# An eight-chunk decoder layer: two groups of row transposes and one copy of probabilities moved in the attention turn's hand-written order

## The reference, cut to what matters

```python
x = x + recurrence(layernorm(x))
q = layernorm(x) @ Wq + bq                      # 16 heads of 32
scores = einsum('bhqd,bhkd->bhqk', q, k) / sqrt(32)
scores = where(causal mask, -inf, scores)
out = einsum('bhqk,bhkd->bhqd', softmax(scores), v)
x = x + out @ Wo + bo
x = x + experts(layernorm(x))                   # top 2 of 4 by x @ gate_W
```

## Time and profile before

| | |
|---|---|
| median of 3 runs | 1167.13 us (1164.18 to 1169.15) |
| the profiled execution's own time | 1170.26 us |
| its span (first to last instruction) | 1168.5 us |
| PE busy | 95% of the span |
| DVE busy | 78% |
| ACT busy | 62% |
| POOL busy | 34% |
| granted TensorE clock | 0.991 of full speed |

### The profile page before, as it was taken

How to read it: one execution, slowest core, us unless ns; L and a number is a source line. 1 busy time by engine, 2 the same in 40 slices (tenths; PEclk the granted TensorE clock), 3 DMA queues, 4 the chain that set the end, 5 groups by cost and what they waited for, 6 DMA issues and landing times.

```text
span 1168.5 us, 24237 instructions
## 1 busy us (share of the span) xinstructions
PE 1108.3 (95%) x6017; PEld 905.0 (77%) x6018; DVE 910.5 (78%) x2172; ACT 722.2 (62%) x2148; POOL 393.4 (34%) x328
## 2 busy tenths in 40 slices
PE   6999999999989999999999888999999999999993
PEld 5888888888877787777777666777888888888882
DVE  6888888887874778878878877877777777777774
ACT  5223332233377777768676644866787787877873
POOL 3000000000034433545536364445534434443432
PEclk9999999999999999999999998999999999999998
DMA  8544545445340133143143377786555454444543
GB/s 261 163 149 159 190 148 173 151 163 207 126 147 1 57 89 111 56 124 100 46 145 90 128 206 219 201 249 152 94 85 81 81 85 80 86 81 81 88 63 40
DMA packets 95316, 144.76 MB, mean 124 GB/s; under 512 B 20864, under 2 KB 37428, under 8 KB 94607
## 3 DMA queue, kind: packets, MB, share of 16 engines
q1 hardware_dynamic: 77338, 106.83, 28.8%
q0 software_dynamic: 17216, 35.73, 17.4%
q10 hardware_dynamic: 693, 1.36, 0.4%
HBM read 82.69 MB, written 64.76 MB: 126 GB/s over the span
## 4 chain that ended last, share of the span: by engine, by line
PE 72%; DVE 9%; issue 7%; DMA 6%; ACT 3%; POOL 2%; DVEq 0%; POOLq 0%; ACTq 0%; SPq 0%
PE banks L1126 27%; PE banks L716 17%; PE banks L928 7%; PE banks L781 6%; DMA out<-rows,scatter_rows 4%; PE banks L893 3%; PE banks L906 3%; PE banks L1154 2%; PE banks L1138 2%; ACT rows L1335 2%; DVE operands L1615 2%; PE banks L917 1%; PE banks L754 1%; DVE rows L1917 1%; ACT operands L1218 1%
## 5 line engine op out<-in xcount | busy, mean ns | idle before, releaser
L1126 PE MATMUL banks<-operands 128*128 x1608 | 390.5, 398 | 9.2 <-ACT operands L1218 5.0
L1126 PEld LDWEIGHTS banks<-operands 128*128 128x128 f32 x1608 | 299.5, 190 | 73.9 <-issue 14.2
L716 PE MATMUL banks<-operands 128*128 128x512 f32 (+2 forms) x1224 | 290.1, 393 | 3.6 <-DVE operands L1615 3.6
L716 PEld LDWEIGHTS banks<-operands 128*128 128x128 f32 (+1 forms) x1224 | 226.1, 192 | 48.3 <-DVE operands L1615 3.7
L1218 ACT ACTIVATE operands<-banks 128x512 fp32r<-128x512 f32 (+1 forms) x232 | 137.6, 602 | 63.4 <-PE banks L807 34.2
L1615 DVE TENSOR_TENSOR operands<-banks,operands 128x512 fp32r<-128x512 f32 (+1 forms) x232 | 156.7, 683 | 15.6 <-ACT operands L1218 12.2
L1335 ACT ACTIVATE rows<-banks,score_shift 128x77 f32<-128x77 f32 x512 | 158.4, 337 | 11.2 <-DVE score_shift L1839 10.9
L2686 POOL DMA_INDIRECT out<-rows,scatter_rows x67 | 106.4, 1588 | 155.3 <-DVE rows L2419 109.7
L1218 ACT ACTIVATE operands<-rows 128x512 fp32r<-128x512 f32 (+2 forms) x77 | 54.0, 710 | 163.6 <-DVE rows L1686 139.4
L1540 ACT ACTIVATE banks<-banks,param_cols 128x128 f32<-128x128 f32 x268 | 99.2, 431 | 82.2 <-PE banks L1154 75.6
L2357 DVE BATCH_NORM_STATS2 moe_stats<-banks 128x6 f32<-128x512 f32 x134 | 93.2, 696 | 37.5 <-PE banks L1126 31.5
(11 more groups left out here) (191 smaller groups left out, 1603.1 us busy)
## 6 DMA issues: line engine op xcount, KB each, us to landing
expert_parts<-operands SPq DMA_DIRECT2D x32, 512.0 KB, 3.0
operands<-expert_parts SPq DMA_DIRECT2D x8, 2048.0 KB, 11.4
rows<-in_x SPq DMA_DIRECT2D x8, 1024.0 KB, 5.5
rows<-in_L_ffn_W SPq DMA_DIRECT2D x32, 256.0 KB, 3.6
x_rows<-rows SPq DMA_DIRECT2D x8, 1024.0 KB, 4.3
rows<-x_rows SPq DMA_DIRECT2D x8, 1024.0 KB, 6.2
xf_rows<-rows SPq DMA_DIRECT2D x32, 256.0 KB
out<-rows SPq DMA_DIRECT2D x32, 256.0 KB
```

Of the source, the lines that this page charges most:

```text
L716: last = nc.tensor.matmul(dst, stationary(a, k), moving(b, k), start=(t == 0 and k == 0), stop=(t == len(terms) - 1 and k == n_k - 1))
L1126: last = nc.tensor.matmul(dst, stationary[:, a, k, :], weights[:, w, bass.ds(e, 1), a2, k, :].rearrange("p e f -> p (e f)"), start=False, ...
```

## The change

Three lists are edited, all inside `b_turn`. On PE, the transposes of x2 go in front of the projection of tile 3, and those of x3 in front of attend(c, 0). On ACT, the high parts of x2 and x3 each go in front of one more tile of exponentials. On DVE, the low part of x2 goes in front of x2_stats(2), x2_add(3) and x2_stats(3); and near the end of the turn the copy of head 3's probabilities of group 3 goes in front of the last part of `slots` and of q_lo(c + 1, 3). No instruction is added or removed, and no DMA is moved.

```diff
@@ PE, b_turn
                 scores(c, 2, (2, 3))
-                x1_to_features(c + 1, c, (1,))
+                x1_to_features(c + 1, c, (1, 2))
                 if back:
                     project(c - 1, c, 3)
-                x1_to_features(c + 1, c, (2,))
+                x1_to_features(c + 1, c, (3,))
                 attend(c, 0)
-                x1_to_features(c + 1, c, (3,))
                 probs_to_keys(c, 1, 0)
@@ ACT, b_turn
                 exp_scores(c, 2, (1,))
+                x1_hi(c + 1, (2,))
                 exp_scores(c, 2, (2,))
-                x1_hi(c + 1, (2,))
+                x1_hi(c + 1, (3,))
                 exp_scores(c, 2, (3,))
-                x1_hi(c + 1, (3,))
                 pT_even(c, 1, 0)
@@ DVE, b_turn
                 if back2:
                     read_positions(c, totals=totals)
+                x1_lo(c + 1, (2,))
                 if back:
                     x2_stats(c - 1, c, 2)
                     x2_add(c - 1, c, 3)
-                x1_lo(c + 1, (2,))
-                if back:
                     x2_stats(c - 1, c, 3)
                 x1_lo(c + 1, (3,))
@@ DVE, b_turn, near its end
                 invert_sums(c + 1, 0)
+                pT_odd(c, 3, 1)
                 if back2:
                     slots(c - 2, c, parts=(2,))
                 q_lo(c + 1, 3)
-                pT_odd(c, 3, 1)
                 max_scores(c + 1, 1, 0)
```

## The result

| | before | changed |
|---|---|---|
| median of 6 runs | 1168.14 us (1163.45 to 1170.20) | 1181.10 us (1178.20 to 1183.26) |
| profiled execution | 1170.26 us | 1180.26 us |
| its span | 1168.5 us | 1178.5 us |
| mean granted TensorE clock | 0.991 | 0.984 |

The ratio is 1.0116, with a 95% interval of 1.0089 to 1.0143: the changed kernel is slower by 13 us, where 3.3 us of gain were forecast.

A forecast was written before the change was run, and what follows sets the result against it. PE, busy 95%, was taken as the bound, idling behind DVE at two places. Six turns at 0.55 us gave 3.3, the swapped copy nothing: 1167.13 - 3.3 = 1163.8 us, range 1158.2 to 1169.4.

The forecast's parts named there:

- x2 didn't hold up the projection: On PE, x2's transposes, now ahead of the projection, find x0 read in time, with 0.08 us to spare; costed at nothing.
- p11: Transposes of probabilities on PE, waiting for x1_lo(3): to start 0.55 us earlier in turn 4, where 1.48 were lost.
- Turn 4 stood for the others: Turn 4's gain of 0.55 us was taken for each of six turns: 3.3 us; turn 1 maybe less, turn 6 more.
- The pair x2_add, x2_stats: Dependent neighbours on DVE, put directly behind each other: 0.85 us from start to start, against 0.60 for independent ones.
- rival 3: On DVE, x2_stats directly behind x2_add costs nothing extra: 1.5 us more gain, 1162.3 us; chance 0.06.
- (1): The whole wait at p11 on PE goes: 8.9 us gained, 1158.2 us; chance 0.12.
- (2): The swapped copy of head 3's probabilities pays too, at attend(c, 3): 5.6 us in all, 1161.5 us; chance 0.07.
- (4): The gain is absorbed by a later PE wait, above all at attend(c, 3): time stays at 1167.1 us; chance 0.14.
- (5): On PE, x2's transposes hold up the projection: slower, 1173 us if 1.75 us late; chance 0.05.
- the 0.99: Part of turn 4's 1.48 us loss shown as PE idle before p11; most of the rest was put before p10.
- The bank argument: At the turn's end, attend(c, 3) needs both the probabilities' copy and q_lo, which frees its bank; swapping them gives 0.
- the bounds I set for this part: Moving head 3's probabilities' copy on DVE was to gain between 0 and 0.70 us a turn at attend(c, 3).

The follow-up runs named there:

- the third experiment: The changed kernel with the last part of slots back in front of the moved probabilities' copy, which stays ahead of q_lo: 0.9964 of the kernel before.
- the copy alone: The kernel before with only the copy of head 3's probabilities moved, the transposes left in place: 1.0141 of the kernel before.
- the two-input form: The changed kernel with the counts' copy written as a tensor_tensor maximum of the counts with themselves: 1182.97 us, one execution, beside a median of 1173.07 before.
- the reduce: The changed kernel, order untouched, with the counts' copy written as a tensor_reduce over one element: 1.0084 of the kernel before.
- the gates twice: The changed kernel with the 32 gate-score matmuls in front of attend(c, 3) issued twice in a row: 1.0086 of the kernel before.

## Why the prediction was wrong

**Right: the transposes.** Each step held in turn 4: x2 didn't hold up the projection, x1_hi(2) and (3) fell where they were put, x1_lo(3) lost its wait for ACT and got one for its place in the queue, p11 came 6.34 us behind x1's transposes for a forecast of 6.37. Turn 4 stood for the others fairly: turn 1 gave less (0.31) and turn 6 more (1.09), both as the prediction said they might, and the six together 3.8 us for 3.3. The pair x2_add, x2_stats took 0.81 from start to start (540.49 to 541.30), near the 0.85 of the earlier trace rows and not the 0.60 of independent neighbours. So the price of the pair, which rival 3 doubted, is there. By itself this half measured 0.9967, against 0.9972 forecast (1163.8 / 1167.13); the closeness of the total is in part luck, since the interval reaches from 0.9946 to 0.9987 and the profiled execution had one turn 3 us long. None of the rivals came about for this half: p11's wait did not go (1), the swap paid nothing (2), the pair had its price (3), the gain was not absorbed (4) and the projection was not held up (5). One small reading was off without harm: before p10 PE lost 0.21 of the 0.49 us that lie outside the 0.99, so not "most"; the rest is the end of p10's own transposes ahead of the idle time.

**Wrong: the copy of head 3's probabilities.** The step that failed is "pT_odd at 556.35, L2026 0.60 later at 556.95, q_lo at 557.29 ... So this part costs nothing and gives nothing". The bank argument in it holds (q_lo is the releaser, and the swap is free, by the third experiment). The 0.10 for L2026 at its new place became 1.89, q_lo began 2.68 us behind pT_odd in turn 2 instead of 0.94, and the wait at attend(c, 3) grew to 2.2 to 2.4 us. What failed is that a step's duration was taken along when the step was moved. The 0.10 us of L2026 in the earlier trace rows belong to the place where POOL stands still: in turn 4 the copy started at 556.35 and POOL at 556.52. I read DVE's list and PE's, and of POOL's only that it isn't edited. It lay beside the moved step all the same, and the bounds I set for this part, "0 and 0.70", excluded a loss without a reason.

A row of the trace before showed what a small instruction that meets POOL can cost:

```profile
538.90 1.26 DVE L1894 TENSOR_SCALAR base_scale<-ln_rstd 128x2 f32<-128x2 f32 x1
```

Two numbers per partition, 1.26 us, behind the start of a POOL instruction at 538.55 that ran to 540.12; the least of the same line was 0.103. With that row the hold could have been priced: POOL's normalisation of 2.25 us starts 0.34 behind the reciprocal, the copy 0.55 behind pT_odd, so the copy ends with POOL, about 1.8 late, and attend(c, 3) with it, in five turns. By this estimate it is 9 us of loss against 3.3 of gain, on the slower side before any talk of the clock. The waits grew by 8.3 us (11.2 less 2.9).

**Not priced at all: the clock.** A wait of PE was costed at its length. In these runs a wait of 2.2 us was followed, in many turns but not all, by 3.4 to 6.8 us at 1.2 GHz, which made it about twice as dear. The waits of 0.5 to 0.7 us at attend(c, 3), and those of 0.9 to 1.0 at p11, had no such cost in turns 3 to 6 of the kernel before.

So the changed kernel is the sum of -3.8 us (p11), 8.3 us (five holds) and some 8 us for four turns' clock (196.2 less four times the 47.0 of a held turn at full clock): about 13, and 13.0 was measured. The last term is an estimate from other kernels' turns; that the wait causes the fall is not shown by an experiment of its own, only that in these profiles the falls in the six turns come behind waits of 1.3 us or more or, once, behind three short ones in a row (0.23, 0.70 and 0.99 us, with the copy alone).

## What to carry to other kernels

When a step is moved in one engine's list, look at what the other engines run at its new place, also those whose lists aren't edited: a duration belongs to an instruction and its neighbours in time, and the greatest duration of the same kind in the trace, beside its least, is the bound. A small instruction on DVE with a copy or tensor_scalar form, or with two SBUF inputs, goes in front of the step that sets POOL going, or takes a form that POOL doesn't hold up. And where a wait of PE grows from half a microsecond to two, count the clock beside the wait.

## What was not expected of the hardware

That the form decides and not the size: with POOL's 2.25 us tensor_tensor at work, a copy of 128 x 4 took 1.89 us, a two-input maximum 1.88 and an addition of a constant 1.72, while a reduce of the same four numbers took 0.14, and the copy of 77 x 512 out of PSUM its usual 0.68. And that the granted clock's fall isn't a fixed companion of the wait: of four turns held alike, all four had a stretch at 1.2 GHz in the changed kernel's profile, three with the two-input form (0.97, 1.00, 0.93, 0.97), and two with the reduce. With the gates twice it was two as well, one of them behind p11.
